# A chain of four attention and four feed-forward layers on one core: the layer of eight experts sends its tokens by a list, and its results are gathered and added batch by batch in the attention behind it

## The chip, the cores and the metric

The kernel runs on one core of one Trainium2 chip. The core has five engines that run their own instruction streams: TensorE (PE; its weight loads appear as PEld), VectorE (DVE), ScalarE (ACT), GpSimd (POOL) and SyncE (SP), which only issues DMAs here. They meet through semaphores. The metric is the device time of one execution in microseconds; lower is better.

## What is computed

The reference runs a state `x` of 16 batches of 128 tokens, 256 numbers each, through eight layers, each of which adds its output to `x`: attention, a layer of 32 experts, an fp8 attention, a layer of eight experts, attention, a ternary feed-forward layer, attention, a ternary feed-forward layer. The change touches the layer of 32 experts in one small place, the layer of eight experts, and the first attention behind it:

```python
# layer of eight experts, on the normalised x
router_logits = jnp.einsum('bsh,he->bse', hidden_states, Wr)
topk_logits, selected = jax.lax.top_k(router_logits, TOP_K)      # TOP_K = 2
router_probs = jax.nn.softmax(topk_logits, axis=-1)
out = jnp.zeros_like(hidden_states)
for e in range(NUM_EXPERTS):                                     # 8
    w_e = jnp.where(selected == e, router_probs, 0.0).sum(axis=-1, keepdims=True)
    g = jnp.einsum('bsh,hi->bsi', hidden_states, Wg[e])
    g = jnp.clip(jax.nn.silu(g), -SWIGLU_LIMIT, SWIGLU_LIMIT)
    u = jnp.einsum('bsh,hi->bsi', hidden_states, Wu[e])
    h = jnp.einsum('bsi,ih->bsh', g * u, Wd[e])
    out = out + h * w_e
# the next layer: x = x + attention(layernorm(x), ctx, ctx), 8 heads of 16, softmax over 256 positions
```

## The kernel before

The program is a list of stages, each with one method per engine, and a barrier of all five engines between two stages. `x` stays in SBUF as `X[128 tokens, 16 batches, 256]`.

**The layer of eight experts, `MoeTop2`.** It works in four groups of four batches. VectorE takes the moments of a group (`moments`), GpSimd the power for the deviation, VectorE normalises (`normalise`, L1957), TensorE transposes (L1827) and computes the router's logits (L1837), VectorE picks the two best experts of each token (`choose`, L1969 to L1988), TensorE counts with masks how many earlier tokens go to the same expert (L1850, L1851), and VectorE turns this into a row for each of the two copies of a token (`slots`, L2007 to L2011). Every expert has a region of 2048 rows in `top_in`, a DRAM buffer of 16384 rows that is cleared to zero by eight DMAs of 2 MB, which SP issues inside the fp8 attention (`clear`). GpSimd scatters the normalised rows into it with 32 indirect DMAs (L2151), two for a batch, as soon as the group's slots are there. VectorE computes from the counts how many tiles of 128 rows each expert fills and which row each of the 39 tiles starts at (`layout`, L2018 to L2039). When all scatters have landed, GpSimd gathers the 39 tiles (L2161) and each goes through TensorE: transpose, the two up projections, transpose, down projection (L1900). VectorE copies the result out of PSUM (`copy_out`, L2078) and SP stores it to `top_out`. After all 39 stores GpSimd gathers for each batch two tiles of rows back (L2172, ring of four) and VectorE adds them to `X` with their probabilities (`add`, L2083 and L2085). Then comes the barrier.

**The attention behind it, `Attention` with layer 2.** It runs on a hand-made scheme of steps: step t = 0 is the first head, the 40 steps before it are a prologue, and batch b starts at step 8b - 40, so batches 0 to 4 start in the prologue and 5 to 15 among the heads (8 heads a batch). A batch's start on VectorE is `bn_stats` (L751) to L755; GpSimd then takes a power (L919); four steps later VectorE normalises into `a_QK` (L765). From step 13 on ACT rounds query and key to a first bf16 part (L901), GpSimd makes the rest and the second and third parts (L930, L932, L934), SP stores the parts (`store_cut`) and, at step 27, loads them back as stacks (`load_stack`). TensorE computes scores from the stacks (L602), VectorE takes the row maxima (L736, 640 of 0.68 us), ACT the exponential. The context is loaded by SP, the weights of the next layer by ACT's queue. GpSimd clears nine value buffers `a_V` before its first step (L908 and L910, a memset to 0 and one to 1 each), and ACT's first copy into a value buffer waits for all nine. Attention layers 0 and 3 use the same class.

**The layer of 32 experts, `MoeTop6`.** It has a list of tokens already: `places` compares each pair's tile number (L1555) and its place in the tile (L1563, 24 operations of 128x128 a group) with a counting row, and TensorE multiplies the two masks (L1320), which gives the token number of each place in each tile.

Names in the profile's rows: `n_` is the layer of eight experts, `m_` the layer of 32, `a_` the attention, `top_in` and `top_out` the DRAM buffers above, `moe_in` the DRAM buffer of normalised rows of the layer of 32 experts.

## Time and profile before

| | us |
|---|---|
| median of three runs | 2559.22 |
| the three runs | 2554.13, 2559.22, 2559.9 |
| profiled execution, its own time | 2561.87 |
| its span in the trace | 2560.1 |
| PE busy | 2031.7 (79%) |
| DVE busy | 1799.2 (70%) |
| ACT busy | 1404.7 (55%) |
| POOL busy | 1214.1 (47%) |
| mean granted clock of TensorE | 0.877 |

The mean shares say little about one stage, since the stages have different limits. The layer of eight experts runs from about 1446 to 1699 us, the attention behind it starts at 1699 us. The table of windows gives for stretches of this part the busy time of each engine, the granted clock and the share of the DMA engines; the timeline gives single instructions with their start, length and, in brackets, how long the engine had been idle before and what ended that.

### The profile page before, as it was taken

What the parts mean: (1) busy time and instruction counts of PE and PEld (TensorE: products, weight loads), DVE (VectorE), ACT (ScalarE), POOL (GpSimd) and SP (SyncE); (2) the same over time, 40 slices, a digit from 0 to 9 for tenths busy, and PEclk for the clock granted to TensorE, in tenths of its full rate; (3) what the DMA queues carried; (4) which work ended last, traced back from release to release, by engine and by line L of the source; (5) the groups of instructions that cost most, each with busy time, mean ns of one, the idle gap of its engine ahead of it and who ended that gap; (6) DMA issues with size and microseconds to landing.
All of it is one profiled execution on the core that took longest, in us unless ns stands there. A gap on an engine that the chain in (4) does not pass through costs nothing. (4 is left out here: it accounts for less than half of the span.)

```text
span 2560.1 us, 42709 instructions
## 1 busy us (share of the span) xinstructions
PE 2031.7 (79%) x13434; PEld 1241.5 (48%) x13434; DVE 1799.2 (70%) x4099; ACT 1404.7 (55%) x3553; POOL 1214.1 (47%) x1425
## 2 busy tenths in 40 slices
PE   6999699996899999999999539708844536787487
PEld 3444356663577767677777426404412223333144
DVE  4899594755798999999997623338837756888254
ACT  1777322541788888888888403205644422677343
POOL 4443003435788888888876363265412212343100
PEclk9999789997999999999999759857876655999599
DMA  4566305772207000000000222259710015676100
GB/s 134 168 173 170 119 1 156 243 241 62 44 20 284 20 18 20 23 16 20 20 9 1 101 87 88 75 167 237 205 60 1 1 49 145 160 189 176 44 1 33
DMA packets 264488, 242.06 MB, mean 95 GB/s; under 512 B 37002, under 2 KB 236141, under 8 KB 263629
## 3 DMA queue, kind: packets, MB, share of 16 engines
q1 hardware_dynamic: 237996, 187.71, 25.2%
q0 software_dynamic: 13776, 36.59, 5.2%
q10 hardware_dynamic: 12496, 15.03, 1.7%
q8 instruction: 114, 1.87, 0.3%
q14 instruction: 106, 0.86, 0.1%
HBM read 141.95 MB, written 98.19 MB: 94 GB/s over the span
## 5 line engine op out<-in xcount | busy, mean ns | idle before, releaser
L736 DVE TENSOR_REDUCE a_nm<-bank 128x2 f32<-128x512 f32 x640 | 408.8, 683 | 36.8 <-PE bank L602 34.6
L844 ACT ACTIVATE a_PT<-bank 128x512 f32<-128x512 f32 x640 | 355.4, 603 | 142.9 <-PE bank L609 128.1
L602 PE MATMUL bank<-a_stack_k,a_stack_q 48*128 48x256 bf16 (+2 forms) x1280 | 262.1, 298 | 99.1 <-DVE a_nm L736 61.1
L2858 PE MATMUL bank<-f_w,f_zc 128*128 128x512 bf16 x1152 | 283.6, 383 | 22.3 <-DVE f_zc L2966 18.1
L3178 POOL TENSOR_TENSOR f_hr<-f_hr,half_pow 128x4 f32<-128x4 f32 x192 | 245.4, 1278 | 85.2 <-DVE f_hr L2975 85.1
L609 PE MATMUL bank<-a_stack_q,a_stack_k 51*128 51x256 bf16 (+2 forms) x1280 | 251.2, 288 | 7.6 <-ACT a_PT L844 7.1
L3070 ACT ACTIVATE f_Pm<-bank,f_nmax 128x128 f32<-128x128 f32 x512 | 182.5, 382 | 73.6 <-DVE f_nmax L2990 72.9
L602 PEld LDWEIGHTS bank<-a_stack_k,a_stack_q 48*128 48x128 bf16 (+2 forms) x1280 | 91.6, 99 | 261.5 <-DVE a_nm L736 179.5
L624 PE MATMUL bank<-a_PT,a_V 128*32 128x256 f32 x2560 | 186.2, 412 | 1.4 <-ACT a_PT L844 1.4
L2858 PEld LDWEIGHTS bank<-f_w,f_zc 128*128 128x128 bf16 x1152 | 112.5, 99 | 122.5 <-issue 25.8
L3167 POOL TENSOR_TENSOR f_cf<-f_cbr,f_cmr 128x516 f32<-128x516 bf16 x128 | 156.9, 1226 | 12.6 <-DVE f_cb L3015 11.0
L2985 DVE TENSOR_TENSOR f_raw<-bank,f_hr 128x512 f32<-128x512 f32 x192 | 131.5, 685 | 42.9 <-POOL f_hr L3178 42.8
L1706 POOL DMA_INDIRECT m_xe<-moe_in,m_token x64 | 75.8, 1184 | 178.6 <-DVE m_token L1584 93.8
L3082 ACT ACTIVATE f_cb<-bank,f_rsmooth 128x128 bf16<-128x128 f32 x512 | 147.1, 377 | 23.8 <-PE bank L2818 23.8
L2975 DVE TENSOR_REDUCE f_hr<-f_sq 128x4 f32<-128x516 f32 x192 | 131.3, 684 | 39.2 <-ACT f_sq L3105 37.2
L3105 ACT ACTIVATE f_sq<-bank 128x512 f32<-128x512 f32 x192 | 116.5, 607 | 62.7 <-PE bank L2858 39.3
L3172 POOL TENSOR_TENSOR f_Pm<-f_Pm,f_rs 128x512 f32<-128x512 f32 x128 | 132.6, 1036 | 23.3 <-DVE f_rs L2995 23.1
L2807 PEld LDWEIGHTS bank<-f_KT,f_QT 128*128 128x128 f32 x1024 | 129.3, 192 | 20.0 <-issue 10.8
L2807 PE MATMUL bank<-f_KT,f_QT 128*128 128x128 f32 x1024 | 135.2, 275 | 0.0
L2818 PE MATMUL bank<-f_PT,f_Vv 128*128 128x256 f32 x512 | 132.1, 381 | 2.3 <-ACT f_cb L3082 2.3
L930 POOL TENSOR_TENSOR a_rest<-a_QK,a_parts 128x512 f32<-128x512 f32 x48 | 55.7, 1161 | 164.0 <-ACT a_parts L901 164.0
L977 POOL DMA_INDIRECT f_rows<-moe_out,slot x96 | 107.5, 1120 | 46.1 <-ACTq L129 29.8
(365 smaller groups left out, 4804.1 us busy)
## 6 DMA issues: line engine op xcount, KB each, us to landing
cut<-a_parts SPq DMA_DIRECT2D x96, 192.0 KB
cut<-a_parts SPq DMA_DIRECT2D x144, 128.0 KB
o<-a_O SPq DMA_DIRECT2D x32, 512.0 KB, 3.7
top_in<-zero SPq DMA_DIRECT2D x8, 2048.0 KB, 19.4
a_stack_q<-cut SPq DMA_DIRECT2D x64, 192.0 KB
a_stack_k<-cut SPq DMA_DIRECT2D x64, 192.0 KB
m_w<-in_w SPq DMA_DIRECT2D x32, 368.0 KB
moe_out<-m_oe ACTq DMA_DIRECT2D x32, 256.0 KB
```

The source lines that it names most:

```text
L602: x = t.matmul(ps[:, n * D:(n + 1) * D], self.stack_q[rows, i, slot, n * P:(n + 1) * P], self.stack_k[rows, i, slot, :], start=True, stop= ...
L609: x = t.matmul(ps[:, n * D:(n + 1) * D], self.stack_k[rows, i, slot, n * P:(n + 1) * P], self.stack_q[rows, i, slot, :], start=True, stop= ...
L624: x = t.matmul(self.k.bank[6][32 * s:32 * s + 32, half], self.V1[:, b % self.NV, m, first + s, :], self.PT[:, (4 * q + s) % 8, m, :], star ...
L736: v.tensor_reduce(self.nm[:, g % 2, :, at % self.J, at // self.J], self.k.bank[h % 3][:, :].rearrange("p (n m) -> p n m", n=2), AX.X, ALU. ...
L844: a.activation(self.PT[:, h % 8, :, :].rearrange("p m n -> p (m n)"), self.k.bank[3 + h % 3][:, :], ACT.Exp).then_inc(self.a_exp.sem, 1)
L2807: x = t.matmul(ps[:, j * P:(j + 1) * P], self.QT[:, cross, h, :], self.KT[:, cross, h // 2, :], start=True, stop=True)
L2858: x = t.matmul(ps[:, :], self.zc[:, b % 2, j, c_, :], self.fp8.w3[:, m, c_, at:at + BANK], start=(m == 0 and c_ == 0), stop=(m == 2 and c_ ...
L3070: x = a.activation(self.Pm[:, i, j * P:(j + 1) * P], ps[:, j * P:(j + 1) * P], ACT.Exp, bias=self.nmax[:, i, j:j + 1], accum_out=self.rs[: ...
L3082: x = a.activation(self.cb[:, u % self.NCB, j * P:(j + 1) * P], ps[:, j * P:(j + 1) * P], ACT.Copy, scale=self.fp8.rsmooth[:, h:h + 1])
L3167: g.tensor_tensor(self.cf[:, :].rearrange("p (r n) -> p r n", r=3), clipped, steps, ALU.add).then_inc(self.g_c.sem, 1)
L3172: g.tensor_tensor(pm, pm, self.rs[:, u % 3, :].unsqueeze(2).to_broadcast([P, self.HPB, P]), ALU.mult).then_inc(self.g_P.sem, 1)
L3178: g.tensor_tensor(f, f, self.k.half_pow[:, 0:self.HPB], ALU.pow).then_inc(self.g_hr.sem, 1)
```

## The change

1. `MoeTop6.places`: the 24 operations at L1563 become one operation over 128x3072, from f32.
2. `MoeTop2`, the way in: the clearing of `top_in` and the scatters are gone. SP stores the normalised rows in order into `moe_in` (four DMAs, between the loads of experts 0 to 3 and 4 to 7). VectorE normalises all groups first, then chooses, and for each group cuts a slot into tile and place and compares the place with a counting row (`at_place`, 128x1024). `list_tokens` adds the first tile of the expert, compares with the 39 tile numbers (1248 elements), multiplies by batch and by lane; 32 matmuls and a transpose on TensorE (`tokens`) give the list, and GpSimd gathers the 39 tiles from `moe_in` by it. TensorE counts one group later.
3. The way out: a new class `Pairs` holds the places, the probabilities and the four row buffers (shared with the results' buffers). GpSimd's 32 gathers and VectorE's 32 additions move into `Attention` layer 2: the gathers of batches 0 and 1 stand before its steps, that of batch b + 2 behind batch b's power; the two additions of a batch stand right before its `bn_stats`.
4. In all three attentions each pair of clearings of a value buffer moves behind the power of its batch, and ACT's copy for batch b waits for its own buffer only.

```diff
+            if self.pairs:
+                self.pairs.add(v, at)
...
-        if b == 0:
-            a.wait_ge(self.g_V.sem, self.g_V.at(2 * self.NV))
+        if b < self.NV:
+            a.wait_ge(self.g_V.sem, self.g_V.at(2 * b + 2))
...
-        for i in range(self.NV):
-            g.memset(self.V1[:, i, :, :, :], 0.0).then_inc(self.g_V.sem, 1)
-            g.wait_ge(self.g_V.sem, self.g_V.at(2 * i + 1))
-            g.memset(self.V1[:, i, :, :, self.hd:self.hd + 1], 1.0).then_inc(self.g_V.sem, 1)
         g.wait_ge(k.v_const.sem, k.v_const.at(3))
+        if self.pairs:
+            self.pairs.gather(g, 0)
+            self.pairs.gather(g, 1)
...
                 g.tensor_tensor(m[:, 3:4], m[:, 2:3], k.half_pow[:, 0:1], ALU.pow).then_inc(self.g_pow.sem, 1)
+                if at < self.NV:
+                    self.clear_V(g, at)
+                if self.pairs and at + 2 < B:
+                    self.pairs.gather(g, at + 2)
...
+    def clear_V(self, g, i):
+        g.memset(self.V1[:, i, :, :, :], 0.0).then_inc(self.g_V.sem, 1)
+        g.wait_ge(self.g_V.sem, self.g_V.at(2 * i + 1))
+        g.memset(self.V1[:, i, :, :, self.hd:self.hd + 1], 1.0).then_inc(self.g_V.sem, 1)
...
-        for n in range(NG * TOP_K):
-            i, j = divmod(n, TOP_K)
-            x = v.tensor_scalar(self.at_place[:, i, j, :], self.count16[:, :], self.cutf[:, 1, i, j:j + 1], None, ALU.is_equal)
-            if n < NG * TOP_K - 1:
-                c.mark(x)
-        x.then_inc(self.v_hot.sem, 1)
+        v.tensor_tensor(self.at_place[:, :, :, :], counting(P), self.spread(self.cutf[:, 1, :, :], P), ALU.is_equal).then_inc(self.v_hot.sem, 1)
...
+    def gather(self, g, b):
+        r = b % self.RR
+        if b == 0:
+            for i in range(self.RO):
+                g.wait_ge(self.d_oe[i].sem, self.d_oe[i].at(self.n_oe[i]))
+        if b >= self.RR:
+            g.wait_ge(self.v_sum.sem, self.v_sum.at(b - self.RR + 1))
+        for j in range(2):
+            at = bass.IndirectOffsetOnAxis(ap=self.place[:, b, j:j + 1], axis=0)
+            g.indirect_dma_start(self.rows[:, r, j, :], None, self.rows_out, at, bounds_check=MoeTop2.NT * P - 1,
+                                 oob_is_err=False).then_inc(self.d_row[r].sem, 16)
+    def add(self, v, b):
+        X, c, r = self.k.X, self.k.dve, b % self.RR
+        v.wait_ge(self.d_row[r].sem, self.d_row[r].at(2 * (b // self.RR + 1)))
+        c.mark(v.scalar_tensor_tensor(X[:, b, :], self.rows[:, r, 0, :], self.pr[:, 2, b:b + 1], X[:, b, :], ALU.mult, ALU.add))
+        c.after()
+        v.scalar_tensor_tensor(X[:, b, :], self.rows[:, r, 1, :], self.pr[:, 3, b:b + 1], X[:, b, :],
+                               ALU.mult, ALU.add).then_inc(self.v_sum.sem, 1)
+        v.wait_ge(self.v_sum.sem, self.v_sum.at(b + 1))
...
-    def clear(self, sp):
-        k, n = self.k, 8
-        rows = self.rows_in.rearrange("(e p n r) d -> e p n (r d)", e=self.NE, p=P, n=n)
-        for e in range(self.NE):
-            sp.dma_start(rows[e], k.zero[:, :].unsqueeze(1).to_broadcast([P, n, FILL])).then_inc(self.d_clear.sem, 16)
...
+        self.load_experts(sp, range(0, 4))
+        for g in range(self.GROUPS):
+            bs = slice(self.NG * g, self.NG * (g + 1))
+            sp.wait_ge(self.v_n.sem, self.v_n.at(g + 1))
+            sp.dma_start(self.rows_in[:, bs, :], self.xn[:, bs, :]).then_inc(self.d_rows.sem, 16)
+        self.load_experts(sp, range(4, self.NE))
...
+    def tokens(self, t):
+        n, last = 2 * self.NT, 2 * B - 1
+        t.wait_ge(self.v_hot.sem, self.v_hot.at(1))
+        for i in range(2 * B):
+            b, j = divmod(i, 2)
+            x = t.matmul(self.k.bank[7][0:n, 0:P], self.in_tile[:, b, j, :, :].rearrange("p m n -> p (m n)"), self.at_place[:, b, j, :],
+                         start=(i == 0), stop=(i == last))
+        x.then_inc(self.p_who.sem, 1)
+        t.wait_ge(self.v_who.sem, self.v_who.at(1))
+        t.transpose(self.k.bank[6][:, 0:n], self.who[:, :], self.k.ident[0:n, 0:n]).then_inc(self.p_list.sem, 1)
...
-        self.moments(v, 0)
-        self.moments(v, 1)
-        self.constants(v)
-        for g in range(self.GROUPS + 2):
+        for g in range(self.GROUPS + 1):
             if g < self.GROUPS:
-                self.normalise(v, g)
-            if g + 2 < self.GROUPS:
-                self.moments(v, g + 2)
-            if 1 <= g <= self.GROUPS:
-                self.choose(v, g - 1)
-            if g >= 2:
-                self.slots(v, g - 2)
-        self.layout(v)
+                self.moments(v, g)
+            if g == 1:
+                self.constants(v)
+            if g:
+                self.normalise(v, g - 1)
+        for g in range(self.GROUPS + 1):
+            if g < self.GROUPS:
+                self.choose(v, g)
+            if g == self.GROUPS:
+                self.layout(v)
+            if g:
+                self.slots(v, g - 1)
+        self.list_tokens(v)
...
-        for b in range(B):
-            self.add(v, b)
...
+        v.wait_ge(self.v_slot.sem, self.v_slot.at(g + 1))
+        c.mark(v.tensor_scalar(self.cut[:, 0, sl, :], self.slot[:, sl, :], 7, None, ALU.logical_shift_right))
+        c.mark(v.tensor_scalar(self.cut[:, 1, sl, :], self.slot[:, sl, :], P - 1, None, ALU.bitwise_and))
+        c.after()
+        c.mark(v.tensor_copy(self.cutf[:, :, sl, :], self.cut[:, :, sl, :]))
+        c.after()
+        c.mark(v.tensor_tensor(self.at_place[:, sl, :, :], self.counting(NG, 2, P), self.spread(self.cutf[:, 1, sl, :], P), ALU.is_equal))
...
+    def list_tokens(self, v):
+        c, NT, tile = self.k.dve, self.NT, self.in_tile
...
+        c.after()
+        self.by_expert(v, slice(0, B), self.tiles[:, 1, :].unsqueeze(1).to_broadcast([P, B, self.NE]))
+        c.mark(v.tensor_tensor(self.cutf[:, 0, :, :], self.cutf[:, 0, :, :], self.slotf[:, :, :], ALU.add))
+        c.after()
+        c.mark(v.tensor_tensor(tile[:, :, :, 0, :], self.counting(B, 2, NT), self.spread(self.cutf[:, 0, :, :], NT), ALU.is_equal))
+        c.after()
+        c.mark(v.tensor_tensor(tile[:, :, :, 1, :], tile[:, :, :, 0, :],
+                               self.spread(self.spread(self.count[:, 0:B], 2), NT), ALU.mult))
+        c.after()
+        v.tensor_scalar(tile[:, :, :, 0, :], tile[:, :, :, 0, :], self.lane[:, 0:1], None, ALU.mult).then_inc(self.v_hot.sem, 1)
+        self.owners(v)
+        v.wait_ge(self.p_who.sem, self.p_who.at(1))
+        v.tensor_copy(self.who[:, :], self.k.bank[7][0:2 * NT, 0:P]).then_inc(self.v_who.sem, 1)
+        v.wait_ge(self.p_list.sem, self.p_list.at(1))
+        v.tensor_copy(self.listed[:, :, :].rearrange("p m n -> p (m n)"), self.k.bank[6][:, 0:2 * NT]).then_inc(self.v_list.sem, 1)
+        v.wait_ge(self.v_list.sem, self.v_list.at(1))
+        v.scalar_tensor_tensor(self.token[:, :], self.listed[:, 1, :], float(P), self.listed[:, 0, :], ALU.mult,
+                               ALU.add).then_inc(self.v_token.sem, 1)
+    def owners(self, v):
...
-        g.wait_ge(self.d_clear.sem, self.d_clear.at(self.NE))
-        for b in range(B):
-            if b % 4 == 0:
-                g.wait_ge(self.v_slot.sem, self.v_slot.at(b // 4 + 1))
-            if b >= 4:
-                g.wait_ge(self.d_scat[b % 4].sem, self.d_scat[b % 4].at(2 * (b // 4)))
-            for j in range(2):
-                at = bass.IndirectOffsetOnAxis(ap=self.slot[:, b, j:j + 1], axis=0)
-                g.indirect_dma_start(self.rows_in, at, self.xn[:, b, :], None, bounds_check=self.NE * self.REGION - 1,
-                                     oob_is_err=False).then_inc(self.d_scat[b % 4].sem, 16)
-        g.wait_ge(self.v_row.sem, self.v_row.at(1))
-        for i in range(4):
-            g.wait_ge(self.d_scat[i].sem, self.d_scat[i].at(2 * (B // 4)))
+        g.wait_ge(self.v_token.sem, self.v_token.at(1))
+        g.wait_ge(self.d_rows.sem, self.d_rows.at(self.GROUPS))
         for j in range(self.NT):
             r = j % self.RX
             if j >= self.RX:
                 g.wait_ge(self.p_xT.sem, self.p_xT.at(j - self.RX + 1))
-            at = bass.IndirectOffsetOnAxis(ap=self.row[:, j:j + 1], axis=0)
-            g.indirect_dma_start(self.xe[:, r, :], None, self.rows_in, at, bounds_check=self.NE * self.REGION - 1,
+            at = bass.IndirectOffsetOnAxis(ap=self.token[:, j:j + 1], axis=0)
+            g.indirect_dma_start(self.xe[:, r, :], None, self.k.xbuf, at, bounds_check=B * P - 1,
                                  oob_is_err=False).then_inc(self.d_xe[r].sem, 16)
-        g.wait_ge(self.v_place.sem, self.v_place.at(1))
-        for r in range(self.RO):
-            g.wait_ge(self.d_oe[r].sem, self.d_oe[r].at(-(-(self.NT - r) // self.RO)))
-        for b in range(B):
-            r = b % self.RR
-            if b >= self.RR:
-                g.wait_ge(self.v_sum.sem, self.v_sum.at(b - self.RR + 1))
-            for j in range(2):
-                at = bass.IndirectOffsetOnAxis(ap=self.place[:, b, j:j + 1], axis=0)
-                g.indirect_dma_start(self.rows[:, r, j, :], None, self.rows_out, at, bounds_check=self.NT * P - 1,
-                                     oob_is_err=False).then_inc(self.d_row[r].sem, 16)
...
-            if b == 4 and self.top2:
-                self.top2.clear(sp)
```

GpSimd at the end of the layer and the start of the attention, before. `n_rstd` is the deviation, `n_xe` a tile of rows, `n_rows` the gathered results, `a_V` a value buffer:

```order
814 L2142 TENSOR_TENSOR n_rstd<-n_rstd,half_pow 128x4 x4
815 L2151 DMA top_in<-n_xn,n_slot 16384x256 x32
816 L2161 DMA n_xe<-top_in,n_row 128x256 x39
817 L2172 DMA n_rows<-top_out,n_place 128x256 x32
818 L908 MEMSET a_V 128x512
819 L910 MEMSET a_V 128x16
820 L908 MEMSET a_V 128x512
```

and now:

```order
814 L2221 TENSOR_TENSOR n_rstd<-n_rstd,half_pow 128x4 x4
815 L2229 DMA n_xe<-moe_in,n_token 128x256 x39
816 L1745 DMA pair_rows<-top_out,pair_place 128x256 x4
817 L918 TENSOR_TENSOR a_mv<-a_mv,half_pow 128x1
818 L946 MEMSET a_V 128x512
819 L948 MEMSET a_V 128x16
820 L1745 DMA pair_rows<-top_out,pair_place 128x256 x2
821 L918 TENSOR_TENSOR a_mv<-a_mv,half_pow 128x1
822 L946 MEMSET a_V 128x512
823 L948 MEMSET a_V 128x16
824 L1745 DMA pair_rows<-top_out,pair_place 128x256 x2
```

The 32 scatters are gone; of the 32 gathers of results four stand first in the attention and the others in pairs between the power and the parts (L933 to L937) of the batches, each with one pair of clearings.

VectorE at the same boundary, before (`n_pr` are the probabilities, `a_stats` and `a_mv` the moments, `a_QK` the normalised rows):

```order
2346 L2083 SCALAR_TENSOR_TENSOR X<-n_rows,n_pr,X 128x256
2347 L2085 SCALAR_TENSOR_TENSOR X<-n_rows,n_pr,X 128x256
2348 L698 MEMSET a_one 3x256
2349 L751 BN_STATS a_stats<-X 128x6
2350 L753 BN_AGGR a_mv<-a_stats 128x2
2351 L755 TENSOR_SCALAR a_mv<-a_mv 128x1
2352 L765 TENSOR_SCALAR a_QK<-X,a_mv 128x256
```

and now:

```order
2327 L2165 COPY pair_rows<-bank 128x256 x3
2328 L696 MEMSET a_one 3x256
2329 L1751 SCALAR_TENSOR_TENSOR X<-pair_rows,pair_pr,X 128x256
2330 L1753 SCALAR_TENSOR_TENSOR X<-pair_rows,pair_pr,X 128x256
2331 L751 BN_STATS a_stats<-X 128x6
2332 L753 BN_AGGR a_mv<-a_stats 128x2
2333 L755 TENSOR_SCALAR a_mv<-a_mv 128x1
2334 L765 TENSOR_SCALAR a_QK<-X,a_mv 128x256
2335 L1751 SCALAR_TENSOR_TENSOR X<-pair_rows,pair_pr,X 128x256
2336 L1753 SCALAR_TENSOR_TENSOR X<-pair_rows,pair_pr,X 128x256
```

The additions no longer stand in a block; the two of a batch stand ahead of its moments.

VectorE at the end of the dispatch, from the counts of tiles to the row numbers and the first tile's product, before:

```order
2179 L2018 TENSOR_SCALAR n_tiles<-bank 128x8
2180 L2020 TENSOR_SCALAR n_tiles<-n_tiles 128x8
2181 L2022 TENSOR_TENSOR n_upto<-n_upto,n_tiles 128x64
2182 L2023 TENSOR_SCALAR n_tiles<-n_tiles 128x8
2183 L2025 TENSOR_REDUCE n_incl<-n_upto 128x8
2184 L2027 TENSOR_TENSOR n_past<-n_incl,n_tile 128x273
2185 L2030 TENSOR_REDUCE n_ownf<-n_past 1x39
2186 L2031 TENSOR_TENSOR n_pastw<-n_past,n_tiles 128x273
2187 L2034 CAST n_own<-n_ownf 1x39
2188 L2035 TENSOR_REDUCE n_rowf<-n_pastw 128x39
2189 L2037 TENSOR_TENSOR n_rowf<-n_rowf,n_tile 128x39
2190 L2039 TENSOR_SCALAR n_row<-n_rowf 128x39
```

and now, from the sum over experts to the token numbers:

```order
2197 L2059 TENSOR_TENSOR n_hotw<-n_hot,n_tiles 128x16x8 x2
2198 L2061 TENSOR_REDUCE n_slotf<-n_hotw 128x32
2199 L2111 TENSOR_TENSOR n_cutf<-n_cutf,n_slotf 128x32
2200 L2113 TENSOR_TENSOR n_in_tile<-n_count,n_cutf 128x32x39
2201 L2115 TENSOR_TENSOR n_in_tile<-n_in_tile,n_count 128x32x39
2202 L2118 TENSOR_SCALAR n_in_tile<-n_in_tile,n_lane 128x32x39
2203 L2131 TENSOR_TENSOR n_past<-n_incl,n_count 1x273
2204 L2134 TENSOR_REDUCE n_ownf<-n_past 1x39
2205 L2136 CAST n_own<-n_ownf 1x39
2206 L2121 COPY n_who<-bank 78x128
2207 L2123 COPY n_listed<-bank 128x78
2208 L2125 SCALAR_TENSOR_TENSOR n_token<-n_listed 128x39
```

The row numbers of `top_in` are replaced by masks (`n_in_tile`), two copies around TensorE's work and the token numbers, all of it ahead of the first tile.

## Rows read from the trace of the kernel before

**Rows 1.** Windows: length, busy PE, PEld, DVE, ACT, POOL, clock, DMA share, GB/s.

```profile
1519.00:1646.00 127.00, 121.75 (x468) 73.61 (x468) 43.55 (x128) 41.06 (x118) 38.96 (x39) 0.96 0.26 80
1646.00:1699.00 53.00, 0.00 (x0) 0.00 (x0) 15.76 (x34) 0.00 (x0) 32.41 (x33) 0.52 0.29 84
1725.00:1751.00 26.00, 17.20 (x67) 6.36 (x66) 25.59 (x51) 6.00 (x12) 11.42 (x20) 0.50 0.84 212
1788.00:1826.00 38.00, 31.36 (x252) 15.85 (x256) 37.75 (x81) 21.72 (x43) 20.60 (x34) 0.81 0.86 224
```

**Rows 2.** Timeline of the dispatch: start us, us, engine, operation [idle before <-releaser].

```profile
1452.10 1.94 PE L1827 MATMUL bank<-ident,n_xn 128*128 128x128 f32 x8 [12.19 <-DVE n_xn L1957]
...
1456.99 3.42 PE L1837 MATMUL bank<-n_wr,n_xnT 128*128 128x8 f32 x16
...
1460.45 0.19 DVE L1969 COPY n_lg<-bank 128x32 f32<-128x32 f32 x1 [3.34 <-PE bank L1837]
...
1463.32 1.38 DVE L1957 TENSOR_SCALAR n_xn<-X,n_mv,n_rstd 128x256 f32<-128x256 f32 x4
...
1474.72 1.07 POOL L2151 DMA_INDIRECT top_in<-n_xn,n_slot  x1 [16.52 <-DVE n_slot L2011]
...
1496.30 0.18 DVE L2039 TENSOR_SCALAR n_row<-n_rowf 128x39 uint32<-128x39 f32 x1
...
1519.05 1.04 POOL L2161 DMA_INDIRECT n_xe<-top_in,n_row  x1 [2.28 <-DMA top_in<-n_xn,n_slot]
```

**Rows 3.** Timeline of the end of the layer and the attention's start.

```profile
1645.50 0.42 DVE L2078 COPY n_oe<-bank 128x256 f32<-128x256 f32 x1 [0.44 <-PE bank L1900]
...
1648.57 1.00 POOL L2172 DMA_INDIRECT n_rows<-top_out,n_place  x1 [27.51 <-DMA top_out<-n_oe]
...
1652.72 0.48 DVE L2083 SCALAR_TENSOR_TENSOR X<-n_rows,n_pr,X 128x256 f32<-128x256 f32 x1 [6.80 <-DMA n_rows<-top_out,n_place]
...
1692.53 0.48 DVE L2085 SCALAR_TENSOR_TENSOR X<-n_rows,n_pr,X 128x256 f32<-128x256 f32 x1
...
1698.76 0.52 POOL L908 MEMSET a_V<- 128x512 f32 x1 [8.57 <-POOLq L129]
1698.76 0.27 DVE L698 MEMSET a_one<- 3x256 bf16 x1 [5.75 <-POOLq L129]
```

**Rows 4.** Timeline of the layer of 32 experts: masks, matmuls of the list, first gather.

```profile
321.78 1.76 DVE L1555 TENSOR_TENSOR m_in_tile<-m_count,m_cutf 128x1536 bf16<-128x1536 f32 x1
...
324.91 3.99 DVE L1563 TENSOR_SCALAR m_at_place<-m_count,m_cutf 128x128 bf16<-128x128 bf16 x24
...
394.89 1.50 PE L1320 MATMUL bank<-m_at_place,m_in_tile 128*128 128x128 bf16 x24
...
400.87 0.23 DVE L1584 SCALAR_TENSOR_TENSOR m_token<-m_who 128x64 uint32<-128x64 f32 x1
...
402.00 1.22 POOL L1706 DMA_INDIRECT m_xe<-moe_in,m_token  x1 [93.78 <-DVE m_token L1584]
```

**Rows 5.** Windows in the fp8 attention, the second beside the clearing.

```profile
740.00:750.00 10.00, 9.36 (x58) 6.50 (x57) 8.63 (x18) 7.39 (x22) 8.79 (x7) 1.00 0.01 3
790.00:800.00 10.00, 9.35 (x58) 6.49 (x57) 8.62 (x18) 7.42 (x22) 8.78 (x7) 1.00 1.05 409
```

**Rows 6.** Timeline of the attention's prologue: GpSimd's powers and TensorE's first scores.

```profile
1715.23 0.54 POOL L919 TENSOR_TENSOR a_mv<-a_mv,half_pow 128x1 f32<-128x1 f32 x1
...
1718.76 0.54 POOL L919 TENSOR_TENSOR a_mv<-a_mv,half_pow 128x1 f32<-128x1 f32 x1
...
1723.90 0.40 PE L602 MATMUL bank<-a_stack_k,a_stack_q 96*128 96x256 bf16 x1 [6.48 <-DMA a_stack_k<-cut]
```

**Rows 7.** VectorE normalising, twice; GpSimd waits 1760 to 1840: total us, times, longest.

```profile
1712.28 1.24 DVE L765 TENSOR_SCALAR a_QK<-X,a_mv 128x256 f32<-128x256 f32 x1 [4.23 <-POOL a_mv L919]
...
1763.29 0.41 DVE L765 TENSOR_SCALAR a_QK<-X,a_mv 128x256 f32<-128x256 f32 x1 [0.97 <-POOL a_mv L919]
...
POOL a_rest L930 <- ACT a_parts L901: 28.8, 8, 5.7
```

173 lines of the change are left out of this document (86 added, 87 removed).

## Prediction

> **What bounds the kernel now.** I first read the table of windows across the layer of eight experts and the attention behind it. From 1519 to 1646 us TensorE is busy 121.75 of 127 us, so the 39 tiles of the layer are TensorE's and the change leaves them alone [rows 1]. From 1646 to 1699 us TensorE does nothing: this stretch is GpSimd's 32 gathers (32.41 us busy, the clearing's start included) and VectorE's 32 additions (15.76) [rows 1]. In the attention the bound changes: from 1725 to 1751 us and from 1788 to 1826 us VectorE is busy 25.59 of 26 and 37.75 of 38 us, so anything put on VectorE there is paid in full [rows 1].
>
> Then the timeline of the dispatch. The first of 32 scatters starts at 1474.72 us; the last is over at 1516.8 (1519.05 less the 2.28 us of waiting shown with it), and only then does the first gather of a tile start, at 1519.05. The row numbers that it uses were ready at 1496.48. So 22.6 us before the first tile belong to scatters alone [rows 2].
>
> Last the boundary. The last result leaves VectorE at 1645.92, the first of the 32 gathers starts at 1648.57, the first sum at 1652.72, the last sum ends at 1693.01, and the attention starts at 1698.7, after 5.75 us of barrier [rows 3].
>
> **The change, part by part.** All sums are made against the profiled execution, 2561.87 us (span 2560.1), which is 2.65 us above the median 2559.22.
>
> *The mask in the layer of 32 experts.* 24 instructions take 3.99 us by the row, 0.166 each. One operation over 3072 elements takes their place. The nearest row of that kind is 1536 elements in 1.76 us, hence with a fixed part of about 0.16 some 1.04 ns an element and 3.36 us for 3072. It saves about 0.5 us in each of the four groups, three of which stand where TensorE waits for VectorE: **-1.5** (between -2 and 0) [rows 4]. The Trainium skill, "VectorE: DVE Perf Modes", section "The perf-mode tier table", puts a bf16 operation with a scalar in the fastest tier and a two-operand fp32 operation in the slowest. By that table alone the 24 would be far cheaper than the one, and the edit would lose about 2.5 us a group, 10 in all; the row with 24 instructions disagrees, since at 128 elements the fixed part of an instruction is nearly all of its 0.166 us. The measurement decides.
>
> *The clearing of 16 MB is gone.* It ran beside the fp8 attention. With it (790 to 800 us, DMA share 1.05, 409 GB/s) TensorE was busy 9.35 of 10 us, without it (740 to 750) 9.36. **0** [rows 5].
>
> *The dispatch.* All normalising now comes first on VectorE, so TensorE can run its transposes (1.94 us a group) and logits (3.42) in a row from about 1452.4 us. Its order is T0, T1 L0, T2 L1, T3 L2 and then the counts of group 0: four times 1.95 and three times 3.42 is 18.1, so the counts come at about 1470.5. From there VectorE is the chain: two choices (2.87 us each, 1460.45 to 1463.32), four slots (five short instructions and three for the cuts, 0.18 to 0.23 each as the short ones in these rows, so 1.6, and a mask of 1024 elements, 1.22 by the price above: 2.8) and the layout (six short ones, 1.3): 5.7 + 11.2 + 1.3 = 18.2, and 1.5 for the waits between engines, gives 1490. The list costs a sum over experts (1.4 for 256 elements twice and a reduction), two operations of 1248 elements (1.46 each by the same price) and one of bf16 with a scalar (at most as much, I take 0.5): 1495. Then 32 matmuls on TensorE. The row has 24 in 1.50 us at full clock, so 2.0, or 4.0 at half clock. TensorE mostly waits in the dispatch, and where it did so elsewhere the granted clock was 0.50 and 0.52 [rows 1]; I take half clock. Copy, transpose, copy and token number are 2, and GpSimd issues 0.9 us after its number, as in the layer before (401.1 to 402.0): the first gather of a tile starts at about 1502 instead of 1519.05: **-17**. Ends: -20 (matmuls at full clock, no waits) and -12 (every hand-over 0.5 us dearer) [rows 2, 4]. What is late next is the list itself, not the normalised rows: their four stores go out by about 1467, 35 us ahead. The second half of the expert weights goes out behind these stores on SP's queue and has 30 us before its first use.
>
> *The stage's end.* Nothing of the gathers stays, so the attention starts one barrier (5.75) after the last result: 1645.92 + 5.75 = 1651.7 in place of 1698.7: **-47** (-48 to -44; the low end if the last stores, 2.65 us to the first gather now, hold up the barrier) [rows 3].
>
> *The attention, start.* GpSimd issues four gathers at 1.31 us, the pitch of the 32 scatters (1474.72 to 1516.8 [rows 2]), in place of nine pairs of clearings at some 0.6 (the first memset takes 0.52, the second is small): 5.2 against 5.6, no loss. But batch 0's moments now wait for rows that land 4.15 us after issue (1648.57 to 1652.72) and for its addition (two times 0.48 with gaps, 1.05). Its power is at 9.4 instead of 5.8: +3.6 with some 2 us for the 3 MB of weights that load at the same time. Behind it GpSimd does one batch every 3.53 us (1715.23 to 1718.76), back to back; each batch now also carries a clearing (0.6) and a gather pair (2.6). The first scores need batches 0 and 1, so 6.4, less about 1 for waits of GpSimd that this fills. **+9** (7 to 14) [rows 3, 6].
>
> *The attention, among the heads.* The additions of 16 batches are 16.8 us of VectorE. Six of them fall where VectorE is full: +6.3. In the other places GpSimd has, of eight batches, 28.8 us of waiting for ACT's parts, 3.6 a batch; a pair of gathers takes 2.6 of it. That leaves 1.0, and a batch that is issued later delays its stores and stack loads; I charge 0.5 for nine batches, 4.5. **+11** (3 to 20) [rows 1, 7].
>
> Sum: -1.5 + 0 - 17 - 47 + 9 + 11 = -45.5. The profiled execution would be 2516.4 us, the median 2.65 lower: **2514 us**.
>
> **Rivals.**
> *A. All covered.* If additions slip into gaps of VectorE in front of the heads and GpSimd's waiting takes the gathers, the attention grows by 9 instead of 20: 2503 us. For it: the 28.8 us of waiting. Against it: 25.59 of 26 us of VectorE.
> *B. Gathers hold VectorE.* One operation of 256 elements that takes 0.41 us alone took 1.24 while GpSimd worked [rows 7]. If each of the 22 gathers that fall among the heads costs VectorE 0.8 us so, that is +17.6: 2532 us. For it: that row. Against it: GpSimd's arithmetic ran beside VectorE there, not a gather. The Trainium skill, "SBUF — State Buffer", section "Who interferes with whom", says that VectorE and GpSimd share one pair of ports under an exclusive lock; by that rule the 22 gathers would cost as in this rival, and the row of 1.24 us agrees with it in direction.
> *C. The dispatch gains nothing.* The list of tokens is a longer chain than the row numbers were. If the list's chain comes out at 1517, with hand-overs of VectorE and TensorE at double price, the change is worth 15 less: 2529 us.
> *D. The work comes back in the attention.* If the gathers set the pace in the prologue and each of 11 batches among the heads takes 2.6 + 1.05 longer, growth is 14 + 40 = 54: 2548 us. It would need both engines in series, and GpSimd's wait says they are not.
> *E. Slower than before.* In 1725 to 1751 us the DMA engines are 84% busy [rows 1]. The addition stands on VectorE's queue ahead of the maxima on which the heads wait, and its rows are asked for two batches ahead. Eight batches fell into 80 us, so that lead is up to 20 us [rows 7]. Landing is 4.15 us now, and up to 20 it costs nothing; what is above is paid once a batch. From 22.9 us on (16 times 2.85 is 45.5, the whole gain) the change loses; at 24 us it costs 64: 2578 us.
> *F. The change doesn't do what it says.* Order and diff show it done; the scatters are gone from GpSimd.
>
> **How the numbers follow.** My case 0.55, A 0.13, B 0.17, C 0.10, D 0.02, E 0.02, F 0.01. A and my case with their edges reach down to 2499 (dispatch -20, boundary -48); B and C reach up to 2532, with an edge of some 6 us 2538. The range is 2499 to 2538. About 0.3% (8 us) is what a measurement of this kernel can tell from no change, so faster means below 2551.5. All but E and F and a part of D are on that side: faster 0.97, same 0.01, slower 0.02.
>
> **What would show it.** In the profile after: the first gather of a tile near 1502 less the 1.5 of the layer before, with no scatter ahead of it; then 127 us of tiles as now; no stretch without TensorE behind it but the barrier; the first scores 34 instead of 25 us after the attention's start (1723.90 less 1698.7 now [rows 6]); VectorE still full in the two stretches. Wrong would be: first scores under 30 or over 40 us after the start, waits of the additions for their gathers among the heads (E), VectorE operations of double length next to gathers (B), or a tile list later than 1510 (C).

## The result and the profile after

The changed kernel takes 2525.82 us (median of four runs, 2521.47 to 2526.82) against 2557.16 us of the kernel before (2554.13 to 2559.9). The ratio is 0.9874 with a 95% interval of 0.9856 to 0.9893: 1.3% faster. The forecast was 2514 us with a range of 2499 to 2538; the direction and the range held, and the gain was 31 us where 45.5 were forecast. The profiled execution took 2525.09 us with a span of 2523.3, 36.8 us below the span of before (the profiled execution of before lay 4.7 us above its median, so the traces differ by more than the medians).

The page of the profile after, part 1 (busy us, share, instructions). TensorE is busy for as long as before, VectorE 15 us more and GpSimd 28 us less.

```profile
PE 2034.0 (81%) x13467; PEld 1242.7 (49%) x13467; DVE 1814.2 (72%) x4020; ACT 1403.7 (56%) x3553; POOL 1186.2 (47%) x1393
```

The barriers between the stages let the 36.8 us be placed. The starts are those of the first VectorE instruction of a stage, in the two traces:

| stage | length before | length after | difference | forecast |
|---|---|---|---|---|
| load and attention, layer 0 (to 297.67, 305.42) | 297.7 | 305.4 | +7.75 | not in the sum |
| 32 experts (to 591.60, 597.86) | 293.9 | 292.4 | -1.5 | -1.5 |
| fp8 attention (to 1445.78, 1451.83) | 854.2 | 854.0 | -0.2 | 0 |
| eight experts (to 1698.76, 1629.62) | 253.0 | 177.8 | -75.2 | -64 |
| attention, layer 2, and the ternary layer (to 2092.40, 2058.44) | 393.6 | 428.8 | +35.2 | +20 |
| attention, layer 3 (to 2409.80, 2372.86) | 317.4 | 314.4 | -3.0 | not in the sum |
| last ternary layer | 150.3 | 150.4 | +0.1 | 0 |

So the layer of eight experts gave 11 us more than forecast, and two attentions took 23 more.

**The dispatch.** The timeline, from the counts of group 0 to the first gather of a tile, answers [rows 2]:

```profile
1475.82 0.19 PE L1899 MATMUL bank<-n_before,n_ones 128*128 128x32 bf16 x1
...
1492.28 1.23 DVE L2079 TENSOR_TENSOR n_at_place<-n_count,n_cutf 128x1024 bf16<-128x1024 f32 x1
...
1494.74 1.46 DVE L2113 TENSOR_TENSOR n_in_tile<-n_count,n_cutf 128x1248 bf16<-128x1248 f32 x1
1496.24 1.46 DVE L2115 TENSOR_TENSOR n_in_tile<-n_in_tile,n_count 128x1248 bf16<-128x1248 bf16 x1
1497.74 0.56 DVE L2118 TENSOR_SCALAR n_in_tile<-n_in_tile,n_lane 128x1248 bf16<-128x1248 bf16 x1
...
1498.35 3.34 PE L1911 MATMUL bank<-n_at_place,n_in_tile 128*78 128x128 bf16 x32 [10.94 <-DVE n_in_tile L2118]
...
1502.67 0.20 DVE L2125 SCALAR_TENSOR_TENSOR n_token<-n_listed 128x39 uint32<-128x39 f32 x1
1503.66 1.09 POOL L2229 DMA_INDIRECT n_xe<-moe_in,n_token  x1 [39.70 <-DVE n_token L2125]
```

The counts come 24.0 us after the stage's start (forecast 24.7), the last mask of places starts at 1492.28, the three masks of tiles take 1.46, 1.46 and 0.56 us, the 32 matmuls 3.34, and GpSimd starts 51.8 us after the stage's start instead of 73.3. That is 21.4 us less, against a forecast of 17. The 4.4 us beyond it are spread over the chain: the counts come 0.7 us earlier, the piece from the counts to the last mask takes 22.5 us where the forecast had 24.5 (it held 1.5 us for waits between engines, and behind the first counts VectorE has none up to the last mask), the matmuls 3.4 instead of 4.0, and the copies and the issue behind them 2.0 instead of 2.9.

**The boundary** answers [rows 3]:

```profile
1628.57 0.42 DVE L2165 COPY pair_rows<-bank 128x256 f32<-128x256 f32 x1 [0.44 <-PE bank L1961]
1629.62 0.27 DVE L696 MEMSET a_one<- 3x256 bf16 x1 [0.63 <-SPq L129]
1631.65 1.00 POOL L1745 DMA_INDIRECT pair_rows<-top_out,pair_place  x1 [27.52 <-DMA top_out<-pair_rows]
...
1639.59 0.49 DVE L1751 SCALAR_TENSOR_TENSOR X<-pair_rows,pair_pr,X 128x256 f32<-128x256 f32 x1 [9.70 <-DMA pair_rows<-top_out,pair_place]
```

The last result leaves VectorE at 1628.99, and 0.63 us later the attention has begun, where before 5.75 us of barrier followed [rows 3]. The wait is not all gone: the first gather still waits until 1631.65 for the last results to land, and its rows are added only at 1639.59, 7.9 us after it, where before a gather was added after 4.15 [rows 3]. The attention's first batch starts its moments 11.0 us after the stage's start, before it was 0.2.

**The attention** in windows (length, busy PE, PEld, DVE, ACT, POOL, clock, DMA share, GB/s), the tiles ahead of it in the first line. They answer [rows 1]:

```profile
1504.00:1630.00 126.00, 120.62 (x468) 73.37 (x468) 42.50 (x122) 40.95 (x118) 38.65 (x39) 0.97 0.27 81
1630.00:1660.00 30.00, 2.73 (x8) 1.16 (x8) 8.52 (x23) 2.15 (x5) 19.27 (x25) 0.52 0.59 202
1660.00:1690.00 30.00, 8.55 (x32) 3.38 (x32) 21.33 (x39) 2.82 (x7) 21.45 (x32) 0.50 1.00 245
1690.00:1730.00 40.00, 33.18 (x228) 16.39 (x226) 34.34 (x64) 20.32 (x42) 29.09 (x46) 0.71 0.81 205
1730.00:1780.00 50.00, 37.42 (x302) 18.83 (x300) 45.45 (x92) 27.53 (x56) 32.42 (x49) 0.83 0.90 219
```

TensorE has next to nothing to do in the first 60 us (2.73 and 8.55 us busy), and among the heads VectorE is busy 34.34 of 40 and 45.45 of 50 us. GpSimd is busy 21.45 of 30 us from 1660 to 1690, and its timeline shows one batch of the prologue:

```profile
1653.16 0.56 POOL L918 TENSOR_TENSOR a_mv<-a_mv,half_pow 128x1 f32<-128x1 f32 x1
1653.68 0.51 POOL L946 MEMSET a_V<- 128x512 f32 x1
1654.25 0.16 POOL L948 MEMSET a_V<- 128x16 f32 x1
1654.99 1.21 POOL L1745 DMA_INDIRECT pair_rows<-top_out,pair_place  x1 [0.58 <-issue]
1656.50 0.99 POOL L1745 DMA_INDIRECT pair_rows<-top_out,pair_place  x1 [0.30 <-issue]
1657.52 1.16 POOL L933 TENSOR_TENSOR a_rest<-a_QK,a_parts 128x512 f32<-128x512 f32 x1
...
1659.43 1.15 POOL L937 TENSOR_TENSOR a_parts<-a_rest,a_parts 128x512 bf16<-128x512 f32 x1
1660.55 0.58 POOL L918 TENSOR_TENSOR a_mv<-a_mv,half_pow 128x1 f32<-128x1 f32 x1
...
1670.56 0.82 PE L600 MATMUL bank<-a_stack_k,a_stack_q 96*128 96x256 bf16 x3 [7.54 <-DMA a_stack_k<-cut]
```

From power to power it is 7.4 us where it was 3.53 [rows 6]: the clearing (0.51 and 0.16), 0.58 us in which nothing is shown, two gathers, and the parts as before (the line left out is their cast, 0.61 us). Four batches in a row have a pitch of 7.3 to 7.4. The first scores come at 1670.56, 40.9 us after the start, before 25.1.

### The profile page after: what moved, and what is told of

Read it like the earlier page. It is cut to its first block and busy times, and to the rows that moved or that the text cites. A ratio compares the mean times of both kernels' runs of the same rounds, so it can differ in the third digit from the quotient of the medians.

```text
span 2523.3 us, 42640 instructions
## 1 busy us (share of the span) xinstructions
PE 2034.0 (81%) x13467; PEld 1242.7 (49%) x13467; DVE 1814.2 (72%) x4020; ACT 1403.7 (56%) x3553; POOL 1186.2 (47%) x1393
## 5 line engine op out<-in xcount | busy, mean ns | idle before, releaser
L2913 PEld LDWEIGHTS bank<-f_w,f_zc 128*128 128x128 bf16 x1152 | 112.2, 99 | 123.0 <-issue 25.4
L2862 PEld LDWEIGHTS bank<-f_KT,f_QT 128*128 128x128 f32 x1024 | 130.0, 192 | 20.1 <-issue 10.8
L2906 PE MATMUL bank<-f_wkv,f_cT 128*128 128x512 f32 x256 | 122.1, 601 | 6.6 <-DMA f_cT<-in_ctx_T 5.8
```

The costliest lines, as they stand in the source:

```text
L2862: x = t.matmul(ps[:, j * P:(j + 1) * P], self.QT[:, cross, h, :], self.KT[:, cross, h // 2, :], start=True, stop=True)
L2913: x = t.matmul(ps[:, :], self.zc[:, b % 2, j, c_, :], self.fp8.w3[:, m, c_, at:at + BANK], start=(m == 0 and c_ == 0), stop=(m == 2 and c_ ...
```

## The experiments

Each length is that of one profiled execution, and most of them move by some us where the code is the same. g_last_on_gpsimd has the attention of the changed kernel unchanged and took 426.4 us for it instead of 428.8. The last attention lies between 310.6 and 316.0 us in the eight kernels that share its code, the fp8 attention between 851.5 and 858.0 in all ten. A difference of up to about 5 us between two stages is therefore not read as an effect. The time to the first scores repeats better: 40.9, 40.7 and 40.4 us in three kernels that gather and clear alike there. The attention is compared in two lengths: from its start to the first scores (the prologue), and from there to the start of the last attention (the heads and the ternary layer).

| kernel | prologue | heads and on | sum |
|---|---|---|---|
| before | 25.1 | 368.5 | 393.6 |
| after | 40.9 | 387.9 | 428.8 |
| a_block_end | 27.0 | 368.8 | 395.8 |
| b_clear_start | 44.8 | 388.0 | 432.8 |
| c_no_gather | 37.8 | 379.0 | 416.8 |
| d_no_add | 40.7 | 376.7 | 417.4 |
| e_vector_clears | 38.6 | 382.0 | 420.6 |
| f_four_up_front | 37.1 | 384.8 | 421.9 |
| h_weights_later | 37.8 | 385.7 | 423.5 |
| g_last_on_gpsimd | 40.4 | 386.0 | 426.4 |

**a_block_end**: the gathers and additions back at the end of the layer, and layer 0 cleared before its steps.

```diff
-            if self.pairs:
-                self.pairs.add(v, at)
...
-                if self.pairs and at + 2 < B:
-                    self.pairs.gather(g, at + 2)
...
             if i == 1:
                 self.places(v)
+        for b in range(B):
+            self.pairs.add(v, b)
...
+        for b in range(B):
+            self.pairs.gather(g, b)
```

> The changed kernel with the 32 gathers and 32 additions put back at the end of the layer of eight experts; the value buffers of the first attention (layer 0) are cleared before its steps as in the kernel before, those of layers 2 and 3 in their steps. The new dispatch stays. Theory 1 (the new waits for the clearings made layer 0 7.75 us longer, where the layer of 32 experts started 305.4 instead of 297.7 us into the span): that start returns to 297.7, give or take 0.5. If layer 0 is longer for another reason, it stays near 305. Theory 2 (gathers and additions make the attention of layer 2 longer, by 35 us up to the start of the last attention: 428.9 against 393.6): with the block out of it the length falls to 393 to 399, the rest being the clearings in the steps; if the clearings do most of it, it stays above 410. The layer of eight experts grows by the block, from 177.7 to about 230 us, and the whole lies at 2530 to 2545.

A single execution gave 2543.82 us. The timeline of VectorE's first and TensorE's first score instruction in the attention:

```profile
1683.76 0.27 DVE L696 MEMSET a_one<- 3x256 bf16 x1 [3.13 <-POOLq L129]
...
1710.75 1.46 PE L600 MATMUL bank<-a_stack_k,a_stack_q 96*128 96x256 bf16 x6 [6.44 <-DMA a_stack_k<-cut]
```

The attention is back at 395.8 us, so gathers and additions make 33 of the 35.2 us; the other 2, which the clearings of layer 2 in their steps may cost, are within the spread. The layer takes 227.7 us, 25.3 less than before with the same way out, which is the dispatch (21.2), the tiles (1.3) and a barrier of 3.13 instead of 5.75 us. Moving the block was thus worth 227.7 - 177.8 = 49.9 us in the layer and took back 33.0 in the attention: 17 of 50 remain. The expectation for the start of the layer of 32 experts (297.7) failed, it came at 305.2. The moments of layer 0's fifth batch, though, start at 60.2 us, as before (60.3), and not at 66.3 as in the changed kernel; what came later is at the stage's end, where this run's clock from 225 to 310 us was 0.77 against 0.84 before. The next kernels bear this out; h_weights_later, which also clears before the steps, has the same late end (303.0 at a clock of 0.75) behind the same early batches.

**b_clear_start**: all three attentions clear before their steps on GpSimd.

```diff
+        if layer in (0, 2, 3):
+            for i in range(self.NV):
+                self.clear_V(g, i)
         g.wait_ge(k.v_const.sem, k.v_const.at(3))
...
-                if at < self.NV:
+                if at < self.NV and not (layer in (0, 2, 3)):
```

> The changed kernel with the clearings of all three attentions back before the steps on GpSimd. Theory: layer 0 gives back 7.75 us, layer 3 loses the 3.0 us that it gained. In layer 2 the nine clearings (5.6 us) stand in front of the first gather, of which 2 us are covered by the wait for the last results, and each of the five batches of the prologue is freed of 0.67 us of clearing and some 0.3 of gap on GpSimd: 3.6 lost, 5 won. Sum about -6: 2519 (2516 to 2522). Rival: if the clearings only filled idle time of GpSimd in all three, the whole stays at 2525.

Measured: 2521.43 us (2520.82 to 2524.14), ratio to before 0.9857 (0.9834 to 0.988). Layer 0 ends at 297.2, layer 3 takes 317.3: both as expected. Layer 2 went the other way: 432.8, 4 us longer instead of 1.4 shorter, all of it in the prologue. The whole lies in the expected range all the same, and its ratio's interval overlaps that of the changed kernel, so a gain over it is not shown. The first gather and the first addition:

```profile
1627.89 1.00 POOL L1748 DMA_INDIRECT pair_rows<-top_out,pair_place  x1 [0.77 <-issue]
...
1637.52 0.48 DVE L1754 SCALAR_TENSOR_TENSOR X<-pair_rows,pair_pr,X 128x256 f32<-128x256 f32 x1 [15.82 <-DMA pair_rows<-top_out,pair_place]
```

The nine clearings stand in front of the first gather and delay the first addition to 16.1 us after the start instead of 10.0. I had set 2 us of them against the wait for the results; in fact 6.5 us pass before the first gather, and batch 0's power comes 6.1 us later than in the changed kernel (18.1 against 11.9). From there to the parts of batch 1, GpSimd wins 3.5 us back, which does not make up for it.

**c_no_gather**: batches 4 to 15 take the rows of batches 0 to 3.

```diff
-                if self.pairs and at + 2 < B:
+                if self.pairs and at + 2 < 4:
...
-        v.wait_ge(self.d_row[r].sem, self.d_row[r].at(2 * (b // self.RR + 1)))
+        v.wait_ge(self.d_row[r].sem, self.d_row[r].at(2))
```

> The changed kernel without the gathers of batches 4 to 15: their additions take the rows that batches 0 to 3 gathered, and do not wait (this leaves out 24 of 32 gathers, so the sums of those batches are other ones). Theory (GpSimd's chain of 7.4 us a batch, of which a pair of gathers takes 2.6 to 3.1, sets the prologue, and gathers also hold up VectorE's additions and GpSimd among the heads): the length from the attention's start to the last attention's start falls from 428.9 to 405 to 412, GpSimd's pitch between powers in the prologue to about 4.4, the additions take 0.48 each everywhere. Rival (the additions on VectorE do it): it falls by less than 10, to 419 or more.

A single execution gave 2517.63 us. The attention takes 416.8 us, 12.0 less (3.1 in the prologue, 8.9 behind it): more than the rival's 10 and less than the theory's 17 to 24. Against g_last_on_gpsimd, with the same attention as the changed kernel, it is 9.6 less. GpSimd's pitch in the prologue fell to 5.3 us, not to the 4.4 that I expected: with no gathers in it GpSimd waits 1.06 us a batch for ACT's parts. The additions did not become short either. Two of them among the heads, without a gather near:

```profile
1700.71 0.85 DVE L1751 SCALAR_TENSOR_TENSOR X<-pair_rows,pair_pr,X 128x256 f32<-128x256 f32 x1
1701.59 1.26 DVE L1753 SCALAR_TENSOR_TENSOR X<-pair_rows,pair_pr,X 128x256 f32<-128x256 f32 x1
```

**d_no_add**: all gathers, no additions.

```diff
-        c.mark(v.scalar_tensor_tensor(X[:, b, :], self.rows[:, r, 0, :], self.pr[:, 2, b:b + 1], X[:, b, :], ALU.mult, ALU.add))
-        c.after()
-        v.scalar_tensor_tensor(X[:, b, :], self.rows[:, r, 1, :], self.pr[:, 3, b:b + 1], X[:, b, :],
-                               ALU.mult, ALU.add).then_inc(self.v_sum.sem, 1)
+        v.tensor_copy(self.pr[:, 0, b:b + 1], self.pr[:, 2, b:b + 1]).then_inc(self.v_sum.sem, 1)
```

> The changed kernel with all gathers but without the 32 additions; one copy of a single column marks a batch as taken (leaves out the sums). Theory (VectorE is full among the heads and not in the prologue): the first scores come at 41.0 less about 2 us after the attention's start, and the length of 428.9 falls by 8 to 14, to 415 to 421. Rival (gathers alone do it, VectorE has room): it falls by less than 4.

A single execution gave 2515.02 us. The attention takes 417.4 us, 11.4 less, as the theory said, and the first scores don't move (40.7):

```profile
1670.06 1.25 PE L600 MATMUL bank<-a_stack_k,a_stack_q 96*128 96x256 bf16 x5 [8.17 <-DMA a_stack_k<-cut]
```

Behind the prologue the two terms roughly add up: 11.2 us without the additions, 8.9 without the gathers, together 20.1, where 19.1 lie between the changed kernel and a_block_end. Taken from g_last_on_gpsimd instead they are 9.3 and 7.1 of 17.2, so each is known to some 2 us. In the prologue neither does it alone: batch 0's power comes 11.9 us after the start there and 1.1 in a_block_end, and no run takes only that wait away.

**e_vector_clears**: layer 0 clears before its steps on GpSimd, layer 2 on VectorE while that waits for the first rows.

```diff
         self.dve_parameters(v)
+        if self.layer == 2:
+            for i in range(self.NV):
+                self.clear_V(v, i)
...
+        if layer == 0:
+            for i in range(self.NV):
+                self.clear_V(g, i)
         g.wait_ge(k.v_const.sem, k.v_const.at(3))
...
-                if at < self.NV:
+                if at < self.NV and not (layer in (2,) or layer == 0):
```

> The changed kernel with the clearings of layer 0 before the steps on GpSimd and those of layer 2 on VectorE before its steps, where VectorE waits 9.7 us for the first rows; layer 3 clears in its steps as now. Theory: layer 0 gives back 8 us; in layer 2 each of the five batches of the prologue is freed of 0.67 us and of the gap of 0.3 behind it on GpSimd, so the pitch of the powers falls from 7.4 to about 6.4 and the first scores come 3 to 5 us earlier than 40.9 after the attention's start: 2513 to 2515. Rival (the pitch is set by something else, ACT's copy or the landing of rows): layer 2 stays at 428.8 and the whole at 2518.

Measured: 2511.78 us (2506.47 to 2515.69), ratio 0.9831 (0.981 to 0.9852): 1 us below the theory's 2513 to 2515. Layer 0 ends at 297.1, and the attention of layer 2 takes 420.6 us, 8.2 less than in the changed kernel. GpSimd's powers in the prologue:

```profile
1650.23 0.58 POOL L924 TENSOR_TENSOR a_mv<-a_mv,half_pow 128x1 f32<-128x1 f32 x1
...
1650.99 1.20 POOL L1751 DMA_INDIRECT pair_rows<-top_out,pair_place  x1 [0.19 <-issue]
...
1656.55 0.56 POOL L924 TENSOR_TENSOR a_mv<-a_mv,half_pow 128x1 f32<-128x1 f32 x1
```

The pitch is 6.3 us instead of 7.4. The first scores come 2.3 us earlier, less than the 3 to 5 that I gave it; the other 5.9 us of the 8.2 lie behind them, which I had not expected and no run explains.

**f_four_up_front**: as e, and four batches' gathers before the steps.

```diff
-            self.pairs.gather(g, 0)
-            self.pairs.gather(g, 1)
+            for b in range(4):
+                self.pairs.gather(g, b)
...
-                if self.pairs and at + 2 < B:
+                if self.pairs and at >= 2 and at + 2 < B:
```

> As e_vector_clears, and the gathers of batches 0 to 3 stand before the steps instead of 0 and 1; the steps of batches 0 and 1 then issue none. GpSimd idles 5.0 us there now, and four gathers take 5.2. Theory (gathers in the chain of parts(0) and parts(1) set the first scores): first scores another 4 to 5 us earlier, at 32 to 34 after the start, whole at 2508 to 2511. Rival (the first scores follow the landing of the first rows and the transfers): first scores move by less than 2.

Measured: 2511.91 us (2505.03 to 2514.76), ratio 0.9822 (0.9797 to 0.9848): not to be told from e. The first scores come 1.5 us earlier than in e, not 4 to 5. The number is the rival's. GpSimd ends the parts of batch 1 at 26.1 us after the start instead of 27.6, and the first scores follow 11.0 us later in both kernels, in the kernel before 8.6. What is left is thus three pieces in a row: batch 0's power at 12.2 us, behind its rows; 13.9 us of GpSimd from there to the parts of batch 1; and 11.0 us for their store and the load of the stacks. Which of them the DMA engines set was not tried apart.

**h_weights_later**: as f, and ACT issues the 3 MB of weights behind the first batch's addition.

```diff
+        if self.pairs:
+            a.wait_ge(self.pairs.v_sum.sem, self.pairs.v_sum.at(1))
         if self.ternary:
             self.ternary.load(a)
```

> As f_four_up_front, and ACT issues the 3 MB of weights of the next layer after the first batch's addition. Theory (the first rows land 7.9 us after their gather instead of 4.15 because they share the DMA engines with these weights): the first addition comes 3 to 4 us earlier, 7 after the attention's start instead of 10, and the first scores with it, whole at 2505 to 2508. Rival (the weights then meet the stores and stacks of the first batches, where DMA is at 1.00): the first addition is earlier, but the first scores are not, and the whole stays at or above f_four_up_front.

Measured: 2507.17 us (2502.21 to 2513.62), ratio 0.9802 (0.9781 to 0.9823). The range overlaps those of e and f, and the attention is not shorter (423.5 against 421.9 and 420.6), so I don't call it faster than these, though the median is where the theory put it. The first addition and GpSimd behind it:

```profile
1634.20 0.48 DVE L1759 SCALAR_TENSOR_TENSOR X<-pair_rows,pair_pr,X 128x256 f32<-128x256 f32 x1
...
1638.98 0.99 POOL L1753 DMA_INDIRECT pair_rows<-top_out,pair_place  x1 [0.30 <-issue]
1639.99 0.60 POOL L926 TENSOR_TENSOR a_mv<-a_mv,half_pow 128x1 f32<-128x1 f32 x1
```

The addition comes 6.5 us after the start instead of 10.0 and 4.4 us after its gather instead of 7.9, so the weights did hold up the first rows (it stands right behind the last clearing, so the rows may have been there before). It brings nothing: GpSimd is at its eight gathers until 1639.97 and takes the power of batch 0 12.3 us after the start, as in f.

**g_last_on_gpsimd**: one small GpSimd operation that waits for the last result, and in the layer of 32 experts the 24 operations again.

```diff
+        g.wait_ge(self.v_oe.sem, self.v_oe.at(self.NT))
+        g.tensor_tensor(self.mv[:, 0, 0:1], self.mv[:, 0, 1:2], self.k.half_pow[:, 0:1], ALU.mult)
...
-        v.tensor_tensor(self.at_place[:, :, :, :], counting(P), self.spread(self.cutf[:, 1, :, :], P), ALU.is_equal).then_inc(self.v_hot.sem, 1)
+        for n in range(NG * TOP_K):
+            i, j = divmod(n, TOP_K)
+            x = v.tensor_scalar(self.at_place[:, i, j, :], self.count16[:, :], self.cutf[:, 1, i, j:j + 1], None, ALU.is_equal)
...
```

> Two separate questions in two stages. (1) The changed kernel with one small GpSimd operation at the end of the layer of eight experts that waits for the last result. The attention started 0.63 us after the last result where GpSimd's last gather was long over, 8.6 us after GpSimd's last operation at both other boundaries (1443.2 to 1451.8; in the kernel before 1689.9 to 1698.7). Theory (the barrier costs some 8.5 us from GpSimd's last operation): the attention starts 8 to 9 us later than 0.63 behind the last result, the layer takes 186 instead of 177.8. Rival (the barrier is cheap behind this layer for another reason): it stays below 2 us. (2) In the layer of 32 experts the 24 operations with a scalar are back in place of one of 3072 elements: that stage takes 293.9 instead of 292.4 us, as in the kernel before.

A single execution gave 2529.71 us. The last result, GpSimd's small operation and the attention's start:

```profile
1633.36 0.42 DVE L2171 COPY pair_rows<-bank 128x256 f32<-128x256 f32 x1 [0.44 <-PE bank L1967]
1633.87 0.19 POOL L2238 TENSOR_TENSOR n_mv<-n_mv,half_pow 128x1 f32<-128x1 f32 x1 [24.95 <-DVE pair_rows L2171]
1637.40 0.27 DVE L696 MEMSET a_one<- 3x256 bf16 x1 [3.62 <-POOLq L129]
```

The wait between the last result and the start is 3.62 us instead of 0.63, and it ends on GpSimd's queue. So a GpSimd instruction at the end of a stage does make the barrier dear, but the 8.5 us of my theory is no constant: it was 3.3 here from the end of that operation and 6.0 in a_block_end (1677.8 to 1683.8). The layer took 182.9 us, between the theory's 186 and the rival. The trace shows what is waited for. At the barrier every engine runs a drain; these are GpSimd's at this boundary (length in ns, then the start), in the kernel before, the changed one and this one:

```profile
L129 POOLq DRAIN  x1: 14932/14932/14932, 1683.7 to 1683.7; - x1
...
L129 POOLq DRAIN  x1: 5552/5552/5552, 1602.9 to 1602.9; - x1
...
L129 POOLq DRAIN  x1: 3466/3466/3466, 1633.8 to 1633.8; - x1
```

In the kernel before it ends at 1698.65, 0.11 us ahead of the attention's start. In the changed kernel it ends at 1608.5, 20 us before VectorE's last result, and so costs nothing. Here it ends at 1637.3, 0.1 us ahead of the start. In a_block_end it took 12.4 us and ended at 1683.65, again 0.11 us ahead.

On the second question: the layer of 32 experts took 292.8 us with the 24 operations; the eight other runs with the one operation lie between 291.9 and 293.0. The difference of 1.5 us between the two first traces is therefore not shown to be the mask.

## Why the prediction held in direction and range, and where its steps were off

**The way in and out of the layer** was sized right and a little small. The dispatch gave 21.4 us instead of 17. The end gave 52.2 instead of 47, and the tiles were 1.5 shorter: together the 75.2. I kept the barrier of 5.75 us as a constant of a boundary, but its last part waits for GpSimd's drain, and GpSimd had nothing left to do. g_last_on_gpsimd shows that one operation there brings 3 us of it back. It is also less of a gain than it looks, since the first gather waits 2.0 us of it for the last stores.

**The mask in the layer of 32 experts** was forecast at -1.5 and the two traces give -1.5, but that is luck: with the 24 operations back, g_last_on_gpsimd has the same length as the kernels with the one. The single operation itself takes 3.35 us, as the forecast had it (3.36).

**The moved clearings in layer 0** are the step that was missing. The change's part 4 touches all three attentions; I followed it only in layer 2. In layer 0 the clearing used to run while the core waited for its first data. The timeline of the changed kernel for batch 1:

```profile
24.11 0.55 POOL L918 TENSOR_TENSOR a_mv<-a_mv,half_pow 128x1 f32<-128x1 f32 x1
...
24.61 0.95 POOL L946 MEMSET a_V<- 128x1024 f32 x1
...
25.61 0.18 POOL L948 MEMSET a_V<- 128x32 f32 x1
...
25.88 0.37 ACT L874 COPY a_V<-bank 128x256 f32<-128x256 f32 x1 [4.86 <-POOL a_V L948]
...
26.30 0.79 PE L665 MATMUL bank<-a_ctx,a_W 128*128 128x256 f32 x1 [4.31 <-ACT a_V L874]
```

ACT's copy waits 4.86 us for the clearing, which stands behind GpSimd's parts of the batch before, and TensorE waits 4.31 us for the copy, which has to free its bank. In the kernel before the same copy was there 5 us earlier:

```profile
20.91 0.37 ACT L874 COPY a_V<-bank 128x256 f32<-128x256 f32 x1 [1.02 <-PE bank L661]
```

The fifth batch's moments start at 66.1 to 66.4 us in the four kernels that clear in the steps and at 60.2 to 60.4 in the six that clear before them. So 6 us of the loss are there in every trace. What the stage's end makes of it depends also on the granted clock of its last part. Where the mean from 225 to 310 us was 0.83 to 0.88, the stage ended at 297.1 to 297.7 us with the clearings ahead and at 303.7 to 305.4 with them in the steps; where it was 0.75 to 0.78, at 303.0 and 305.2 against 310.3. The move cost layer 0 between 5 and 8 us. In layer 3 the kernels that clear in the steps take 310.6 to 316.0 us, the two that clear before them 317.4 and 317.3; that looks like a gain, but the eight with the same code differ by 5.4 us among themselves, so it is not shown.

**The prologue of layer 2** was forecast at +9 and measured at +15.8. The mechanism was right (GpSimd back to back, first scores late), its terms too small. Batch 0's power came 11.9 us after the start (5.7 before) instead of 9.4, since rows took 7.9 us and not 6.1 to be added, behind a wait of 2.0 that I had left out. From there to the parts of batch 1 it was 19.0 us against 10.8 before (power at 1704.47, parts done at 1715.27), 8.2 more where I had 5.4; each batch carries 0.57 to 0.58 us between clearing and gather that I didn't know of. The stacks then took 1.4 longer. With 40.9 us, the first scores lie just beyond the 40 that the prediction named as a sign of being wrong.

**Among the heads** +11 was forecast, +19.4 measured. 18.1 of it lie between the first scores and the last row maximum of the heads, 136.0 us before and 154.1 after. VectorE's idle time in that stretch fell only from 24.2 to 21.3 us, while the 22 additions of batches 5 to 15 take 19.7 us of it, where I had 10.6 in all and charged 6.3. The timeline of the changed kernel shows why, an addition in the prologue first, then two among the heads:

```profile
1647.74 0.48 DVE L1751 SCALAR_TENSOR_TENSOR X<-pair_rows,pair_pr,X 128x256 f32<-128x256 f32 x1 [0.61 <-DMA pair_rows<-top_out,pair_place]
1647.76 1.04 POOL L1745 DMA_INDIRECT pair_rows<-top_out,pair_place  x1 [0.57 <-issue]
...
1730.27 1.16 POOL L933 TENSOR_TENSOR a_rest<-a_QK,a_parts 128x512 f32<-128x512 f32 x1 [1.87 <-ACT a_parts L901]
1730.60 1.11 DVE L1751 SCALAR_TENSOR_TENSOR X<-pair_rows,pair_pr,X 128x256 f32<-128x256 f32 x1
1731.50 0.69 POOL L935 CAST a_parts<-a_rest 128x512 bf16<-128x512 f32 x1
1731.75 0.71 DVE L1753 SCALAR_TENSOR_TENSOR X<-pair_rows,pair_pr,X 128x256 f32<-128x256 f32 x1
```

Of the 32 additions of the changed kernel, the 12 that ran alone or beside a clearing or a gather took 0.47 to 0.49 us, the 20 beside GpSimd's arithmetic 0.71 to 1.81 (the longest began beside a gather and ran into the arithmetic behind it). Not all of this time is on the path: without the additions (d_no_add) 11.2 us come back (9.3 against g_last_on_gpsimd), and VectorE then idles 25.4 us. The gathers are 8.9 (c_no_gather; 7.1 against g_last_on_gpsimd), where I had 4.5. The granted clock over this stretch was 0.80 before and 0.77 after; what part TensorE's lower clock has in the growth, no run separates.

**The rivals.** A (all covered) and C (no gain in the dispatch) are refuted by the numbers above; the attention grew by 35 us, between my 20 and the 54 of D. B was right that VectorE is held beside GpSimd and wrong on by what: it is the arithmetic, not the gathers. Beside a gather an addition stays at 0.48 us, and the normalising of 256 elements, B's own row, at 0.40 to 0.41. (Also, 18 gathers and not 22 stand behind the powers of batches 5 to 13.) Without the gathers the 22 additions take 16.4 us instead of 19.7, but in g_last_on_gpsimd, with all gathers and the same attention, they take 16.9, so that difference is how they happen to fall beside GpSimd's arithmetic. The Trainium skill, "SBUF — State Buffer", section "Who interferes with whom", says that a VectorE operation with two inputs from SBUF and a GpSimd operation that reads SBUF exclude each other. The trace agrees in kind: the additions, which have two such inputs, grow beside GpSimd's arithmetic (0.71 to 1.81 us instead of 0.48), while the moments, with one input, stay at 0.43 us beside it. E (rows land later than the additions ask for them) did not happen. VectorE's waits from 1690 to 1780 us (in total, number and longest) are these two, none of them for a gather:

```profile
DVE a_nm L734 <- PE bank L600: 6.3, 5, 2.4
DVE a_On L804 <- DMA a_den<-r: 2.6, 1, 2.6
```

**Luck in the sum.** The total came out 12 us from the forecast because two larger errors stood against each other: the layer of eight experts gave 11 us more than forecast, and two attentions took 23 more, 8 of them in a layer that the sum did not contain.

What is still open: what the 0.57 us before a gather behind a clearing are (0.19 behind a power alone, in kernel e), what sets the length of GpSimd's drain, and by what way the gathers lengthen the heads, since neither the additions nor the normalising take longer beside one.

## What to carry to other kernels

A block of gathers and additions that stands alone between two stages is worth moving into the next stage, but count it on the engines that carry it there: here 33 of 50 us came back, because GpSimd set the prologue and VectorE the heads. When a helper that three stages use is changed, follow it through each of them; the same move cost 5 to 8 us in one and made no difference clear of the spread in the two others. Work that an engine can do while it waits for the first data belongs there, on whichever engine waits: with the clearings put back in layer 0 and on VectorE in layer 2, the kernel runs at 2511.78 us, 14 less than the changed one (the ratios to before, 0.9831 and 0.9874, differ by 11 us, and their intervals lie just apart).

## What the runs showed of the hardware that I had not expected

- The barrier between two stages waits for GpSimd's drain: behind VectorE's last operation it took 5.75 us (kernel before) and 3.13 us (a_block_end) where GpSimd had issued gathers up to the end, 3.62 with one small GpSimd operation at the end, and 0.63 where the drain had ended 20 us earlier.
- An addition with two inputs from SBUF took 0.47 to 0.49 us alone, beside a clearing and beside a gather, and 0.71 to 1.81 beside GpSimd's arithmetic; two together 1.5 to 2.5 instead of 0.96.
- An indirect gather of 128 rows was added 4.15 us after its issue at a DMA share of 0.24 (kernel before) and 7.9 us after it beside 3 MB of weights, at 1.01; with these weights issued later it was 4.4 us, at 0.53.
- In the prologue a gather started 0.57 to 0.61 us after a clearing on GpSimd, 0.30 us after another gather and, in kernel e, 0.19 us after a power.
